# Where the low part of the transposed x is formed: VectorE from PSUM instead of GpSimd from SBUF

## The chip, the cores and the metric

The kernel runs on one core of a Trainium2 chip. The time is the device time of one execution in microseconds (us); the median of three executions of the kernel before is 827.89 us. Engines are called TensorE, VectorE, ScalarE, GpSimd and SyncE; in the rows of the profile they are PE (with PEld, its weight loads), DVE, ACT, POOL and SP.

## The reference

x has 32 batches of 256 tokens of 128 features. Three layers follow one another, each added to x:

```python
x = x + 0.5 * ffn(layernorm(x), router_w, w1, w2)      # stream f1
x = x + attn(layernorm(x), W_qkv, W_out)               # stream at
x = x + 0.5 * ffn(layernorm(x), router_w, w1, w2)      # stream f2

# ffn: 8 experts of widths 4 x 128 and 4 x 256, all computed, the best two of a token weighted
probs = sigmoid(x @ router_w.T); topw, sel = top_k(probs, 2); topw /= topw.sum() + 1e-20
h = square(relu(x @ w1[e])); y = h @ w2[e]; out = sum over e of y * combine[e]
# attn: linear attention, 16 heads of 8, with rotary embedding and the feature map elu + 1
```

## The kernel before

The tokens are worked through in 16 groups of 512 tokens (two batches). Each group goes through the streams f1, at and f2. One pass `iteration(t, par)` of the software pipeline, written out by hand for every engine, works on different groups in the different streams: f1 forms the inputs of group t + 2, attention those of group t - 1, and f2 those of group t + 2 - 5. t runs from -3 to 22. Up to t = 3 only f1 has work among the two ffn streams (the ramp), from t = 14 only f2 (the drain); the ten passes between have both.

For precision a product of two float32 matrices is made of three products in TensorE's fp32r format: high part by high part, low by high, high by low. So the transposed and normalised x of a group needs a high part `x_hi` (the value rounded to fp32r) and a low part `x_lo` (the value minus `x_hi`), each 128 x 512. They are made so, for each of the three streams:

1. TensorE (`transpose`) writes the four transposed tiles into PSUM bank 0, called `tp` (L474).
2. ScalarE (`evacuate_x`) copies `tp` to `xT` in SBUF (L721), once `x_lo` of the group before in line has been formed, since all streams share one `xT`.
3. VectorE (`high_part`) casts `xT` to `x_hi` (L978).
4. GpSimd (`low_part`) subtracts `x_hi` from `xT` and gives `x_lo` (L876).

For the ffn streams TensorE (`logits`, L493) then multiplies `xT` by the router's weights and writes the result into the same bank `tp`. ScalarE takes the exponential of it (`exp_logits`, L730 and L734). The router's weights of the tokens are worked out on VectorE, with a square root on GpSimd (`root_of_weights`, L882), turned round through `tp` again (`weight_rows`, L483), written to DRAM, and broadcast by SyncE's DMAs from there to `g_all`, four pieces to a group.

The hidden layer has 12 chunks of 128 units to a group and stream. A pass has 24 places. In the passes with both streams each place has one chunk; where a stream is alone its chunks stand at every second place. A chunk goes: three matmuls on TensorE (`up`, L512 to L514) into one of two banks; VectorE multiplies by the router's weights (`weighted`, L1060, `hid`); ScalarE squares (L752) and rounds to `h_hi` (L763); GpSimd forms `h_lo` (`remainders`, L888); nine places later three matmuls `down` (L530 to L532) add it up.

Each engine does its list strictly in the written order. What matters here:

- TensorE: transpose f1, places 0 to 2, `logits` f1, places 3 to 8, transpose at, places 9 to 11, transpose f2, places 12 to 14, q, `logits` f2, and so on.
- VectorE: `weighted(t, 0)`, `high_part` f1, `weighted(t, 1)`, ..., `mean_variance` f1 after place 4; `high_part` at after place 10; `high_part` f2 after place 12. The first `weighted` of a stream waits for the first piece of `g_all` of its group.
- ScalarE: `exp_logits` f1 stands ahead of `squares(t, 0)`, and `exp_logits` f2 ahead of `squares(t, 4)`.
- GpSimd: `low_part` f1 between the `h_lo` of places 22 and 23 of the pass before; `inv_std` f1 (L864 to L869, 1/std of the layernorm of group t + 3) after the `h_lo` of place 1; `low_part` at after place 7, f2 after place 10.

Of the kernel before, what the change touches and what calls it, by code (L numbers as in the profile page):

```python
# [27 lines left out]
F32 = mybir.dt.float32  # L28
F32R = mybir.dt.float32r
ALU = mybir.AluOpType  # L30
ACT = mybir.ActivationFunctionType
# [5 lines left out]
BG = 2  # L37
# [26 lines left out]
SHIFT = 5  # L64
T_FIRST, T_LAST = -3, NG + SHIFT

class Step:
# [14 lines left out]
    @property  # L82
    def last(self):
        return self.c + self.a * (self.trips - 1)

    @property
    def value(self):
        return self.i * self.a + self.c


def first(v):
    return v.c if isinstance(v, Step) else v
# [10 lines left out]
def due(v):  # L103

    assert (first(v) > 0) == (last(v) > 0)
    return first(v) > 0


def live(n):

    return first(n) >= 0 and last(n) < NG


def first_time(stream, n):

    return stream and not isinstance(n, Step) and n == 0


def done(n):

    if last(n) <= 0:
        return 0
    if first(n) >= NG:
        return NG
    assert first(n) >= 0 and last(n) <= NG
    return n
# [66 lines left out]
def build(nc, x_in, wqkv, wout, router, w1, w2, const, out, rows):  # L193
    ctx = ExitStack()
    with ctx:
        def sb(name, shape, dt=F32):
            return ctx.enter_context(nc.sbuf_tensor(name, shape, dt))

        def sem(name):
            return ctx.enter_context(nc.semaphore(name))  # L200
# [29 lines left out]
        xT = sb("xT", [P, NTOK])  # L230
        xT = {s: xT for s in STREAMS}
        nx = {"f1": 2, "at": 1, "f2": 2}
        x_hi = {s: [sb(f"x_hi_{s}{u}", [P, NTOK], F32R) for u in range(nx[s])] for s in STREAMS}
        x_lo = {s: [sb(f"x_lo_{s}{u}", [P, NTOK], F32R) for u in range(nx[s])] for s in STREAMS}
# [52 lines left out]
        tp = bank[0]  # L287
# [16 lines left out]
        def per(name, keys):  # L304
            return {s: sem(f"s_{name}_{s}") for s in keys}
# [8 lines left out]
        s_xT = per("xT", STREAMS)  # L314
        s_hi = per("hi", STREAMS)
        s_lo = per("lo", STREAMS)
# [28 lines left out]
        A = {n: sem(f"s_a_{n}") for n in names}  # L345
# [104 lines left out]
        def _(pe):  # L450
            mm = nc.tensor.matmul

            def tp_free(t, pos):

                n = [done(m + (pos > k)) for k, m in
                     enumerate((t + 2, t + 1 - SHIFT, t - 1, t + 2 - SHIFT, t + 2))]
                if due(n[0]):
                    pe.wait_ge(s_ex["f1"], value(n[0]))
                if due(n[1]):
                    pe.wait_ge(s_gr["f2"], value(n[1]))  # L460
                if due(n[2]):
                    pe.wait_ge(s_xT["at"], value(n[2]))
                if due(n[3]):
                    pe.wait_ge(s_ex["f2"], value(n[3]))
                if due(n[4]):
                    pe.wait_ge(s_gr["f1"], value(n[4]))
# [19 lines left out]
            def logits(s, n):  # L486
                if not live(n):
                    return
                pe.wait_ge(s_xT[s], value(n + 1))
                if first_time(s == "f1", n):  # L490
                    pe.wait_ge(s_router, 16)
                for k in range(TG):
                    i = mm(tp[:, k * P:k * P + PAD], xT[s][:, k * P:(k + 1) * P], router_sb[:], start=True, stop=True)  # L493
                i.then_inc(s_logit[s], 1)
# [192 lines left out]
        def _(act):  # L687
            fn = nc.scalar.activation
# [23 lines left out]
            def evacuate_x(s, n, t, pos):  # L712
                if not live(n):
                    return
                act.wait_ge(s_t[s], value(n + 1))

                for q, m in (("f1", t + 2), ("at", t - 1), ("f2", t + 2 - SHIFT)):
                    m = done(m + 1 if STREAMS.index(q) < pos else m)
                    if due(m):
                        act.wait_ge(s_lo[q], value(m))  # L720
                fn(xT[s][:], tp[:], ACT.Copy).then_inc(s_xT[s], 1)  # L721

            def exp_logits(s, n):
                if not live(n):
# [122 lines left out]
        @block.gpsimd  # L847
        def _(pool):
            gp = nc.gpsimd
            gp.memset(router_sb[:], 0.0).then_inc(s_zero, 1)  # L850
            gp.memset(c_eps[:], EPS)
            gp.memset(c_mhalf[:], -0.5)
            gp.memset(c_half[:], 0.5)
            gp.memset(c_one[:], 1.0)
            gp.memset(c_cut[:], -ROOT_CUT)
            gp.memset(c_mone[:], -1.0).then_inc(s_pconst, 1)
            pool.wait_ge(s_pconst, 1)

            def inv_std(s, n):

                if not live(n):
                    return
                pool.wait_ge(s_mv[s], value(n + 1))
                gp.tensor_tensor(ve[s][:], mv[s][:, :, 1], c_eps[:], ALU.add).then_inc(s_ve[s], 1)  # L864
                gp.tensor_tensor(nm[s][:], mv[s][:, :, 0], c_mone[:], ALU.mult).then_inc(s_ve[s], 1)
                pool.wait_ge(s_ve[s], value(n * 2 + 2))
                gp.tensor_tensor(rstd[s][:], ve[s][:], c_mhalf[:], ALU.pow).then_inc(s_rstd[s], 1)
                pool.wait_ge(s_rstd[s], value(n + 1))
                gp.tensor_tensor(nbias[s][:], nm[s][:], rstd[s][:], ALU.mult).then_inc(s_nb[s], 1)  # L869

            def low_part(s, n, par):
                if not live(n):
                    return
                u = par if nx[s] == 2 else 0
                pool.wait_ge(s_hi[s], value(n + 1))
                gp.tensor_tensor(x_lo[s][u][:], xT[s][:], x_hi[s][u][:].bitcast(F32), ALU.subtract).then_inc(s_lo[s], 1)  # L876

            def root_of_weights(s, n):
                if not live(n):
                    return  # L880
                pool.wait_ge(s_cwt[s], value(n + 1))
                gp.tensor_tensor(root[s][:], cwt[s][:], c_half[:], ALU.pow).then_inc(s_root[s], 1)  # L882

            def remainders(t, *places):
                for place in places:
                    for s, n, c, _ in chunks(t, place):
                        pool.wait_ge(s_hhi[s], value(n * NC + c + 1))
                        gp.tensor_tensor(h_lo[:, c, :], hid[:, c % STAGE, :], h_hi[:, c, :].bitcast(F32),  # L888
                                         ALU.subtract).then_inc(s_hlo[s], 1)

            def iteration(t, par):
                remainders(t - 1, 21, 22)
                low_part("f1", t + 2, par)
                remainders(t - 1, 23)
                if first_time(True, t + 2):
                    pool.wait_ge(s_w2hi, 1)
                    gp.tensor_tensor(w2_lo[:], w2_raw.rearrange("p (c d) -> p c d", c=NC),
                                     w2_hi[:].bitcast(F32), ALU.subtract).then_inc(s_w2lo, 1)
                remainders(t, 0, 1)
                inv_std("f1", t + 3)  # L900
                remainders(t, 2, 3, 4, 5, 6)
                root_of_weights("f1", t + 2)
                remainders(t, 7)
                low_part("at", t - 1, 0)
                remainders(t, 8, 9, 10)
                low_part("f2", t + 2 - SHIFT, (par + SHIFT) % 2)
                remainders(t, 11)
                remainders(t, 12, 13, 14, 15)
                inv_std("at", t)
                remainders(t, 16, 17, 18)  # L910
                root_of_weights("f2", t + 2 - SHIFT)
                remainders(t, 19)
                inv_std("f2", t + 3 - SHIFT)
                remainders(t, 20)

            pipeline(pool, iteration)


        @block.vector
        def _(dve):  # L920
            v = nc.vector
# [48 lines left out]
                    i = v.bn_aggr(mv[s][:, k, :], bn[s][:, k, :])  # L970
                i.then_inc(s_mv[s], 1)

            def high_part(s, n, par):
                if not live(n):
                    return
                u = par if nx[s] == 2 else 0
                dve.wait_ge(s_xT[s], value(n + 1))
                v.tensor_copy(x_hi[s][u][:], xT[s][:]).then_inc(s_hi[s], 1)  # L978


            def take_sigmoid(s, n):

# [179 lines left out]
            def iteration(t, par):  # L1162
                p2 = (par + SHIFT) % 2
                n1, n2, n2_last = t + 2, t + 2 - SHIFT, t + 1 - SHIFT
# [4 lines left out]
                k_features(t - 2)  # L1169
                q_features(t - 2)  # L1170
                weighted(t, 0)
                high_part("f1", n1, par)
                spread_roots("f2", n2_last, 0)
                weighted(t, 1)
                spread_roots("f2", n2_last, 1)
# [21 lines left out]
                weighted(t, 9)  # L1197
                normalise(t - 2, 2)
                weighted(t, 10)
                high_part("at", t - 1, 0)  # L1200
                choose_two("f1", n1)
                weighted(t, 11)
                weighted(t, 12)
                high_part("f2", n2, p2)
                spread_roots("f1", n1, 0)
                weighted(t, 13)
                spread_roots("f1", n1, 1)
# [62 lines left out]
```

## Time and profile before

| what | us |
|---|---|
| median of 3 executions | 827.89 (826.98 to 828.34) |
| the profiled execution | 823.68 |
| its span, first to last instruction | 821.5 |
| TensorE busy | 737.2 (90%) |
| GpSimd busy | 685.2 (83%) |
| ScalarE busy | 599.2 (73%) |
| VectorE busy | 588.3 (72%) |
| mean granted TensorE clock | 0.978 of full |

Busy time is the time in which the engine had an instruction under way. The profiled execution has 2.2 us outside its span.

### The profile page before, as it was taken

How to read it: one execution, taken by the hardware profiler on the slowest of the kernel's cores; microseconds unless marked ns; L12 is line 12 of the kernel's file. 1: busy time of each engine (PE TensorE's matmuls, PEld its weight loads, DVE VectorE, ACT ScalarE, POOL GpSimd, SP SyncE). 2: the span in 40 equal slices, each digit the busy share in tenths (PEclk: the TensorE clock that was granted, in tenths of full speed). 3: DMA queues.
4: the chain of work that ended last, by engine and by line, in shares of the span. 5: the costliest groups of instructions: out<-in, count | busy, mean ns of one | idle time of the engine just before them, and what ended most of it. 6: DMA issues, size and time to landing. Idle time of an engine off the chain costs nothing.

```text
span 821.5 us, 14132 instructions
## 1 busy us (share of the span) xinstructions
PE 737.2 (90%) x3648; PEld 598.1 (73%) x3648; DVE 588.3 (72%) x1820; ACT 599.2 (73%) x1219; POOL 685.2 (83%) x668
## 2 busy tenths in 40 slices
PE   1679888889999999999899998999999989789887
PEld 1457666767887888878687886878887868667665
DVE  3454678777879798887679687787888577676553
ACT  3567686667787879787687877788877765766765
POOL 4587868869999999999799997999989877675876
PEclk9998999989999999999999999999999999989999
DMA  5443023023233331312333230223333303303330
GB/s 173 167 156 115 28 104 104 1 103 104 104 105 116 104 118 67 107 56 106 108 103 116 103 116 21 107 92 103 117 104 117 116 2 104 94 24 117 116 116 26
DMA packets 31009, 79.25 MB, mean 96 GB/s; under 512 B 3296, under 2 KB 14304, under 8 KB 30944
## 3 DMA queue, kind: packets, MB, share of 16 engines
q1 hardware_dynamic: 28672, 76.03, 27.2%
q10 hardware_dynamic: 2272, 2.51, 0.9%
q8 instruction: 22, 0.36, 0.2%
q14 instruction: 43, 0.35, 0.1%
HBM read 73.81 MB, written 4.72 MB: 96 GB/s over the span
## 4 chain that ended last, share of the span: by engine, by line
PE 45%; POOL 15%; DVE 13%; issue 12%; ACT 10%; DMA 4%; DVEq 0%; POOLq 0%; ACTq 0%; SPq 0%
POOL h_lo L888 9%; PE bank L512 6%; PE bank L530 5%; PE bank L514 5%; PE bank L513 5%; PE bank L531 5%; PE bank L532 5%; DVE hid L1060 4%; ACT h_hi L763 3%; PE bank L563 3%; DMA g_all_f<-rows_f 3%; PE bank L493 2%; ACT hid L752 2%; PE bank L614 2%; ACT xn_f L709 2%
## 5 line engine op out<-in xcount | busy, mean ns | idle before, releaser
L888 POOL TENSOR_TENSOR h_lo<-hid,h_hi 128x512 fp32r<-128x512 f32 x384 | 493.8, 1309 | 97.0 <-ACT h_hi L763 96.3
L1060 DVE SCALAR_TENSOR_TENSOR hid<-bank,g_all_f 128x512 f32<-128x512 f32 x384 | 262.2, 684 | 155.2 <-PE bank L514 121.9
L752 ACT ACTIVATE hid<-hid 128x512 f32<-128x512 f32 x384 | 228.8, 621 | 47.9 <-DVE hid L1060 47.3
L763 ACT ACTIVATE h_hi<-hid 128x512 fp32r<-128x512 f32 x384 | 225.5, 620 | 4.3
L512 PE MATMUL bank<-x_hi_f,w_hi 128*128 128x512 f32 x384 | 165.7, 431 | 21.5 <-DVE hid L1060 20.3
L530 PE MATMUL bank<-h_hi,w_hi 128*128 128x512 f32 x384 | 156.9, 409 | 17.8 <-ACT yT L774 10.6
L531 PE MATMUL bank<-h_lo,w_hi 128*128 128x512 f32 x384 | 153.9, 401 | 0.0
L514 PE MATMUL bank<-x_hi_f,w_lo 128*128 128x512 f32 x384 | 153.7, 400 | 0.0
L532 PE MATMUL bank<-h_hi,w_lo 128*128 128x512 f32 x384 | 153.4, 399 | 0.0
L513 PE MATMUL bank<-x_lo_f,w_hi 128*128 128x512 f32 x384 | 152.9, 398 | 0.0
L512 PEld LDWEIGHTS bank<-x_hi_f,w_hi 128*128 128x128 f32 x384 | 73.9, 192 | 48.0 <-DVE hid L1060 29.7
L530 PEld LDWEIGHTS bank<-h_hi,w_hi 128*128 128x128 f32 x384 | 73.8, 192 | 40.9 <-POOL h_lo L888 14.6
L514 PEld LDWEIGHTS bank<-x_hi_f,w_lo 128*128 128x128 f32 x384 | 73.3, 191 | 17.9
L532 PEld LDWEIGHTS bank<-h_hi,w_lo 128*128 128x128 f32 x384 | 73.5, 192 | 17.1
L531 PEld LDWEIGHTS bank<-h_lo,w_hi 128*128 128x128 f32 x384 | 73.8, 192 | 15.9
L513 PEld LDWEIGHTS bank<-x_lo_f,w_hi 128*128 128x128 f32 x384 | 73.9, 193 | 11.1
L709 ACT ACTIVATE xn_f<-x_sb,nbias_f,rstd_f 128x128 f32<-128x128 f32 (+1 forms) x128 | 52.4, 481 | 11.5 <-POOL nbias_f L869 11.5
L876 POOL TENSOR_TENSOR x_lo_f<-xT,x_hi_f 128x512 fp32r<-128x512 f32 x32 | 41.4, 1292 | 18.7 <-DVE x_hi_f L978 18.7
L882 POOL TENSOR_TENSOR root_f<-cwt_f,c_half 128x8 f32<-128x8 f32 x32 | 53.5, 1672 | 0.0
L721 ACT ACTIVATE xT<-bank 128x512 f32<-128x512 f32 x48 | 28.4, 593 | 31.8 <-PE bank L474 21.2
L978 DVE CAST x_hi_f<-xT 128x512 fp32r<-128x512 f32 x32 | 21.9, 683 | 31.6 <-ACT xT L721 31.6
L730 ACT ACTIVATE ex_f<-bank 128x32 f32<-128x32 f32 x32 | 6.4, 199 | 50.4 <-PE bank L493 50.4
(106 smaller groups left out, 1055.2 us busy)
## 6 DMA issues: line engine op xcount, KB each, us to landing
g_all_f<-rows_f SPq DMA_DIRECT2D x128, 512.0 KB, 5.2
x_sb<-in_x SPq DMA_DIRECT2D x16, 256.0 KB, 3.8
out_x<-x_sb SPq DMA_DIRECT2D x16, 256.0 KB, 6.8
g_all_f<-in_w ACTq DMA_DIRECT2D x2, 768.0 KB, 7.2
con<-in_const ACTq DMA_DIRECT2D x1, 652.0 KB, 7.4
rows_f<-g_row_f SPq DMA_DIRECT2D x32, 16.0 KB, 1.4
g_all_f<-in_wqkv ACTq DMA_DIRECT2D x1, 192.0 KB, 9.2
wout_sb<-in_wout ACTq DMA_DIRECT2D x1, 64.0 KB, 6.9
```

Source lines behind the costliest of these rows:

```text
L512: mm(o, w1_hi[:, w], x_hi[s][u][:], start=True, stop=False)
L513: mm(o, w1_hi[:, w], x_lo[s][u][:], start=False, stop=False)
L514: mm(o, w1_lo[:, w], x_hi[s][u][:], start=False, stop=True).then_inc(s_p1[s], 1)
L530: mm(o, w2_hi[:, c, :], h_hi[:, c, :], start=(c == 0), stop=False)
L531: mm(o, w2_hi[:, c, :], h_lo[:, c, :], start=False, stop=False)
L532: i = mm(o, w2_lo[:, c, :], h_hi[:, c, :], start=False, stop=(c == NC - 1))
L709: i = fn(xn[s][:, k, :], tile, ACT.Identity, bias=nbias[s][:, k:k + 1], scale=rstd[s][:, k:k + 1])
L752: fn(h, h, ACT.Square).then_inc(s_sq[s], 1)
L763: fn(h_hi[:, c, :], hid[:, c % STAGE, :], ACT.Copy).then_inc(s_hhi[s], 1)
L882: gp.tensor_tensor(root[s][:], cwt[s][:], c_half[:], ALU.pow).then_inc(s_root[s], 1)
L888: gp.tensor_tensor(h_lo[:, c, :], hid[:, c % STAGE, :], h_hi[:, c, :].bitcast(F32), ALU.subtract).then_inc(s_hlo[s], 1)
L1060: v.scalar_tensor_tensor(hid[:, c % STAGE, :], hp[c % 2][:], 0.0, g_all[s][:, EXPERT[c], :], ALU.max, ALU.mult).then_inc(s_z[s], 1)
```

## The change

- `x_lo` is now formed by VectorE: it subtracts `x_hi` from the PSUM bank `tp` itself, right behind the place where it made `x_hi`. GpSimd's `low_part` is gone.
- In the stream at, ScalarE writes the rounded `x_hi` straight from `tp`, instead of `xT`; VectorE's cast of that stream is gone. ScalarE then waits for the key and value products of the attention group before, which read `x_hi`.
- Since `tp` is now read by VectorE too, `logits` waits for `x_lo` of its stream and group, and the users of `tp` that come after the transposes of the stream at wait for its `x_lo` in place of its `xT`.

```diff
                 if due(n[2]):
-                    pe.wait_ge(s_xT["at"], value(n[2]))
+                    pe.wait_ge(s_lo["at"], value(n[2]))
...
                 pe.wait_ge(s_xT[s], value(n + 1))
+                pe.wait_ge(s_lo[s], value(n + 1))
                 if first_time(s == "f1", n):
...
-                fn(xT[s][:], tp[:], ACT.Copy).then_inc(s_xT[s], 1)
+                if s == "at":
+                    if due(n):
+                        act.wait_ge(A["kv"], value(n * BG))
+                    fn(x_hi[s][0][:], tp[:], ACT.Copy).then_inc(s_hi[s], 1)
+                else:
+                    fn(xT[s][:], tp[:], ACT.Copy).then_inc(s_xT[s], 1)
...
-            def low_part(s, n, par):
-                if not live(n):
-                    return
-                u = par if nx[s] == 2 else 0
-                pool.wait_ge(s_hi[s], value(n + 1))
-                gp.tensor_tensor(x_lo[s][u][:], xT[s][:], x_hi[s][u][:].bitcast(F32), ALU.subtract).then_inc(s_lo[s], 1)
-
...
-                low_part("f1", t + 2, par)
...
-                low_part("at", t - 1, 0)
...
-                low_part("f2", t + 2 - SHIFT, (par + SHIFT) % 2)
...
-            def high_part(s, n, par):
+            def split_x(s, n, par):
                 if not live(n):
                     return
                 u = par if nx[s] == 2 else 0
-                dve.wait_ge(s_xT[s], value(n + 1))
-                v.tensor_copy(x_hi[s][u][:], xT[s][:]).then_inc(s_hi[s], 1)
-
+                if s != "at":
+                    dve.wait_ge(s_xT[s], value(n + 1))
+                    v.tensor_copy(x_hi[s][u][:], xT[s][:]).then_inc(s_hi[s], 1)
+                dve.wait_ge(s_hi[s], value(n + 1))
+                v.tensor_tensor(x_lo[s][u][:], tp[:], x_hi[s][u][:].bitcast(F32), ALU.subtract).then_inc(s_lo[s], 1)
...
-                high_part("f1", n1, par)
+                split_x("f1", n1, par)
...
-                high_part("at", t - 1, 0)
+                split_x("at", t - 1, 0)
...
-                high_part("f2", n2, p2)
+                split_x("f2", n2, p2)
```

## Rows read from the trace of the kernel before

**Rows 1.** Windows: stretch, busy us (instructions) of PE, PEld, DVE, ACT, POOL, granted clock, DMA

```profile
65.00:68.00 3.00, 3.00 (x10) 2.40 (x9) 0.82 (x2) 1.26 (x2) 3.00 (x3) 0.50 0.21 71
...
240.00:280.00 40.00, 39.47 (x203) 32.64 (x202) 33.16 (x109) 31.70 (x69) 38.52 (x39) 1.00 0.22 75
```

**Rows 2.** Who waited for whom: total us, times, longest

```profile
PE bank L512 <- DVE hid L1060: 20.3, 26, 3.6
...
PE bank L530 <- POOL h_lo L888: 7.2, 10, 2.7
...
PEld bank L563 <- POOL x_lo_at L876: 0.7, 2, 0.4
```

**Rows 3.** Instructions by line, shapes apart: busy us, mean ns

```profile
L876 POOL TENSOR_TENSOR x_lo_f<-xT,x_hi_f 128x512 fp32r<-128x512 f32 x32 | 41.4, 1292 | 18.7 <-DVE x_hi_f L978 18.7
...
L876 POOL TENSOR_TENSOR x_lo_at<-xT,x_hi_at 128x512 fp32r<-128x512 f32 x16 | 20.7, 1292 | 0.0
```

**Rows 4.** Single lines: duration ns min/median/max, first and last start

```profile
L978 DVE CAST x_hi_f<-xT x32: 409/717/1514, 14.9 to 775.0; 128x512 fp32r<-128x512 f32 x32
L978 DVE CAST x_hi_at<-xT x16: 415/418/1539, 92.4 to 714.5; 128x512 fp32r<-128x512 f32 x16
...
L1077 DVE TENSOR_TENSOR qa<-bank,con x16: 672/676/682, 96.4 to 719.3; 128x512 f32<-128x512 f32 x16
```

**Rows 5.** Timeline, a pass with both streams, 264 to 290 us: start, us, instruction [idle before]

```profile
264.44 0.50 DVE L978 CAST x_hi_f<-xT 128x512 fp32r<-128x512 f32 x1
...
264.57 0.50 PE L512 MATMUL bank<-x_hi_f,w_hi 128*128 128x512 f32 x1 [0.38 <-DVE hid L1060]
...
266.97 1.03 PE L493 MATMUL bank<-router_sb,xT 128*128 128x96 f32 x8
...
286.45 0.60 ACT L721 ACTIVATE xT<-bank 128x512 f32<-128x512 f32 x1 [0.68 <-POOL x_lo_at L876]
...
287.08 0.74 DVE L978 CAST x_hi_f<-xT 128x512 fp32r<-128x512 f32 x1 [2.12 <-ACT xT L721]
...
289.04 1.02 PE L493 MATMUL bank<-router_sb,xT 128*128 128x96 f32 x8
```

**Rows 6.** Timeline of the ramp, pass t = 0, 51 to 63 us

```profile
51.84 1.03 PE L493 MATMUL bank<-router_sb,xT 128*128 128x96 f32 x8
...
53.20 0.32 ACT L734 ACTIVATE odds_f<-ex_f,c_one 128x32 f32<-128x32 f32 x1
...
54.62 0.69 DVE L1060 SCALAR_TENSOR_TENSOR hid<-bank,g_all_f 128x512 f32<-128x512 f32 x1 [5.09 <-DMA g_all_f<-rows_f]
...
55.22 0.42 DVE L978 CAST x_hi_f<-xT 128x512 fp32r<-128x512 f32 x1
55.34 0.63 ACT L752 ACTIVATE hid<-hid 128x512 f32<-128x512 f32 x1 [1.82 <-DVE hid L1060]
...
58.77 0.20 POOL L864 TENSOR_TENSOR ve_f<-mv_f,c_eps 128x4 f32<-128x4 f32 x1
...
62.78 0.77 PE L530 MATMUL bank<-h_hi,w_hi 128*128 128x512 f32 x1 [3.66 <-ACT yT L774]
```

**Rows 7.** Timeline of passes t = 1 and t = 2: logits, cast, first square

```profile
79.15 1.02 PE L493 MATMUL bank<-router_sb,xT 128*128 128x96 f32 x8
...
80.90 0.71 DVE L978 CAST x_hi_f<-xT 128x512 fp32r<-128x512 f32 x1
...
81.02 0.64 ACT L752 ACTIVATE hid<-hid 128x512 f32<-128x512 f32 x1 [0.19 <-DVE hid L1060]
...
108.60 1.51 DVE L978 CAST x_hi_f<-xT 128x512 fp32r<-128x512 f32 x1
...
109.16 1.03 PE L493 MATMUL bank<-router_sb,xT 128*128 128x96 f32 x8
```

**Rows 8.** Timeline of the last router pass, 772 to 776 us

```profile
772.86 1.03 PE L493 MATMUL bank<-router_sb,xT 128*128 128x96 f32 x8
...
775.03 0.42 DVE L978 CAST x_hi_f<-xT 128x512 fp32r<-128x512 f32 x1
```

## The prediction

> **What bounds the kernel now.** I read the busy time by stretches first. In a stretch of the ten passes with both streams TensorE has 39.47 us busy of 40, GpSimd 38.52, VectorE 33.16 and ScalarE 31.70 [rows 1]. So in the middle of the run TensorE sets the pace, and GpSimd stands only a little behind it. Then the waits: in the whole run TensorE waits 7.2 us for GpSimd's `h_lo` ahead of L530, its weight loads 0.7 us for `x_lo` of the stream at, and 20.3 us for VectorE's `hid` ahead of L512 [rows 2]. What GpSimd costs TensorE directly is small, whatever its busy share.
>
> The timeline shows where the rest is. In the ramp and the drain a pass is one chain of single steps, with TensorE idle in it: logits, exponential on ScalarE, square and rounding of the first chunk, `h_lo` and 1/std on GpSimd, the next norm and `yT` on ScalarE, and TensorE, which had waited 3.66 us for that [rows 6]. There a late step is paid in full. The reader should see in rows 6 above all that TensorE does the logits at 51.84, ScalarE is done with the exponential at 53.52, and only then, at 54.62, does VectorE get past its wait of 5.09 us for the broadcast of the router's weights. The cast to `x_hi` stands behind that wait, at 55.22. Nobody but GpSimd's `low_part` needed it earlier.
>
> **The change, part by part.** *GpSimd.* It loses 32 + 16 subtractions of 1292 ns, 41.4 + 20.7 = 62.1 us, 3.9 us in a full pass [rows 3]. TensorE can get back from this at most what it waits for GpSimd, 7.2 + 0.7 = 7.9 us if every such wait went [rows 2]. Only few of these waits stand behind a subtraction: I take 1 us, the queue of `h_lo`, root and `x_lo_at` ahead of q in the second attention pass, and keep 0 and 7.9 as ends.
>
> *VectorE.* It gains 48 subtractions with one operand in PSUM. The trace has none; the nearest row is the multiplication of a bank by a constant of the same size, 676 ns, never below 672 or above 682 [rows 4]. I take 0.68 us, and 0.07 us for its wait for the cast just ahead. It loses 16 casts of the stream at, 415 to 1539 ns [rows 4]. In a full pass that is 3 x 0.68 = 2.0 us more, less 0.4 to 1.5. The casts' spread comes from GpSimd: a cast from SBUF that meets one of its 1.3 us subtractions stands until that is done, the multiplication from PSUM never does [rows 4]. I take it that the subtraction is not held up either; if it were, it would cost up to 1539 - 415 = 1124 ns more where it meets one, which is kept as an end of the range for the waits in the ramp. The Trainium skill has a rule on this (SBUF — State Buffer, SBUF: two separate sides): VectorE and GpSimd share a port pair under an exclusive lock, which VectorE needs in its two-port mode or with two SBUF inputs. By that rule the subtraction, with one input in SBUF, is free of the lock, and its 0.68 us would stand; a design that kept the subtraction in SBUF on VectorE would not have that. The row of L1077 agrees.
>
> *ScalarE.* It copies as many times as before, with another output type. I take nothing: the wait for the old key and value products is over half a pass old when it is reached, and the rounding copy to `h_hi` costs as much as the square beside it.
>
> *TensorE.* This is the part that costs. `logits` had to wait for `xT` only; it now waits for `x_lo`, because it overwrites the bank that VectorE still reads. Behind it on TensorE stand the next `down` and `up` chunks, behind them `hid` and VectorE's statistics. On ScalarE `exp_logits` waits for it, and behind that, in order, stand all squares of the pass. On the path to GpSimd's 1/std the squares come first.
>
> In the passes with both streams there is slack. f1: the cast ends at 264.94, `x_lo` at 264.94 + 0.75 = 265.69, the logits start at 266.97, 1.3 us later. f2: 287.82 + 0.75 = 288.57 against 289.04, 0.47 us; besides, ScalarE's copy had waited 0.68 us for GpSimd's `x_lo_at` and now comes that much earlier, so the slack grows to about 1.1 us [rows 5]. The transposes of f2 wait for `x_lo` of at, about 1.3 us ahead of need. TensorE's own bubble in such a pass is 0.38 us behind the first `hid` [rows 5]; with the ten passes it could give 4 us at most, and nothing here removes its cause, the attention features ahead of that `hid`. I take 0, with -4 and +7 as ends (the latter if f2 loses 0.7 us in each of ten passes).
>
> In the ramp there is none. From the start of the logits to the end of `odds` takes 53.52 - 51.84 = 1.68, so the first square can start 1.7 us after `x_lo` is ready [rows 6].
> - t = 0: `x_lo` at 55.22 + 0.42 + 0.75 = 56.39, first square at 58.1 instead of 55.34: +2.75 [rows 6].
> - t = -1: the same pattern (logits at 28.3, broadcast landed at 30.2): +2.75.
> - t = 1: 80.90 + 0.71 + 0.75 = 82.36, square at 84.06 instead of 81.02: +3.0 [rows 7].
> - t = 2: 108.60 + 1.51 + 0.75 = 110.86, logits due at 109.16; ScalarE's squares followed at once: +1.7 [rows 7].
> - t = 3: the same with a cast of 1.14: +1.3.
>
> The sum for the ramp is 11.5 us. In the drain the last router pass has the pattern of t = 0: the logits at 772.86 wait for 775.03 + 0.42 + 0.75 = 776.2 [rows 8], first square +2.75. The pass before it loses 0.9, and in two passes the transposes of f2 wait 0.5 each for `x_lo` of at, together 1.9. All in all 11.5 + 2.75 + 1.9 = 16.2 us. Against it stand the 1 us of GpSimd's queue and, as an estimate, 2 us of delays that fall into waits still there (of the 3.66 and similar): the delay of one step is not always that of the pass. That leaves +13.2 us: the profiled 823.7 would become 836.9. The median of the runs lies 4.2 above the profiled execution, so 827.9 + 13.2 = 841 us.
>
> *The clock.* After TensorE had waited 3.66 us at 62.78 it was granted 0.50, the 1.2 GHz level, through 65 to 68 us [rows 1, 6], and its matmuls ran at half pace. With the change its idle time in t = -1, 0 and 1 is cut differently: about 4.5 us idle ahead of the logits, then work, then the old wait. If each of the four large waits brings one more such stretch, of 5 us at half pace, that is 4 x 2.5 = 10 us more. This is in the range, not in the sum. A rule of the Trainium skill speaks for it (TensorE: Matmul & The Clock Gate, Part 1: The HAM clock gate): idleness lets the gate fall to 1.2 GHz, and activity releases it. By the trace it fell at such a wait; whether the split wait makes more or fewer falls no row shows.
>
> **The rivals.**
> *Slower by about 1.6%* is the forecast, with the waits of the logits paid on the chain. Chance 0.68.
> *Slower by much more*: the same, with the extra half-clock stretches or with VectorE as the late engine in every full pass: 841 + 10 = 851 us or 841 + 7 = 848. For it: rows 1 show the clock falling after such a wait. Against it: the slacks of rows 5. Chance 0.14.
> *The waits are absorbed*: TensorE waits in these passes anyway, so a logits that starts late only moves its idle time, and GpSimd's relief pays the rest. That holds if the first square, not the logits, waits for something later. It doesn't by rows 6 to 8, where the square starts within 0.1 us of VectorE's `hid`, but the steps behind could have slack unseen: +0 to +3, about 829 us. Chance 0.08, half of it within 0.2%.
> *Faster*: GpSimd at 38.5 of 40 us is the true bound of the full passes, and what the rows name as waits for VectorE comes from it at one remove (held-up casts and features). Then a full pass wins the 0.38 us and more, ten passes 4 us, and the ramp part of the 7.9 us, while the logits wait costs less than 3 us in all: 827.9 - 4 - 4 + 3 = 823 us. It decides if VectorE reaches the cast before the logits are due; in rows 6 to 8 it reaches it 0.6 us before to 3.4 us after. Chance 0.10.
>
> **How the numbers follow.** The likeliest case gives 841 us, its own range 835 to 847. To hold 8 in 10 the range reaches up to the clock case and down to where most of the delay is absorbed: 832 to 851. A difference of 0.2% (1.7 us) is about what a measurement of this kernel can tell from none. Slower by more: 0.68 + 0.14 + 0.04 = 0.86; within: 0.04; faster: 0.10.
>
> **What would show it.** In the profile after: the logits of t = -1, 0 and 1 begin right after VectorE's subtraction and TensorE waits for it, some 3 to 4.5 us each; `odds` and the first square follow 1.7 us later. The subtraction takes 0.68 us everywhere. GpSimd falls to about 623 us busy, VectorE rises to about 588 + 33 - 13 = 608. A full pass stays as long as before. The prediction is wrong if full passes get shorter by more than 0.4 us each, if the subtraction is held up, or if the ramp ends as early as before though its logits wait.

## The result, and the profile after

The median of 20 executions is 835.77 us (831.44 to 842.31), against 828.26 us of the kernel before, measured beside it in 20 executions. The ratio is 1.0099, with a 95% interval of 1.0078 to 1.0119: slower by 8.2 us (6.5 to 9.9). Forecast were +13.2 us and a range of 832 to 851. The profiled execution took 834.58 us, its span 832.8.

The page of the kernel after, busy time and two of its groups, with the idle time of the engine ahead of each:

```profile
PE 739.5 (89%) x3648; PEld 599.9 (72%) x3648; DVE 601.9 (72%) x1852; ACT 596.7 (72%) x1219; POOL 622.6 (75%) x620
...
L494 PE MATMUL bank<-router_sb,xT 128*128 128x96 f32 x256 | 36.5, 289 | 18.4 <-DVE x_lo_f L977 16.5 <-issue 1.9
...
L977 DVE TENSOR_TENSOR x_lo_f<-bank,x_hi_f 128x512 fp32r<-128x512 f32 x32 | 22.1, 692 | 1.1
```

GpSimd has lost 63 us of busy time, VectorE gained 14. GpSimd's work is gone as forecast, and the kernel is slower: its busy share had cost little. What is new is the first group's idle time. TensorE now waits 16.5 us ahead of the logits (L494, L493 before) for VectorE's `x_lo`. The timeline says where:

```profile
31.81 1.99 PE L494 MATMUL bank<-router_sb,xT 128*128 128x96 f32 x8 [3.53 <-DVE x_lo_f L977]
58.70 1.10 PE L494 MATMUL bank<-router_sb,xT 128*128 128x96 f32 x8 [3.71 <-DVE x_lo_f L977]
85.66 1.10 PE L494 MATMUL bank<-router_sb,xT 128*128 128x96 f32 x8 [3.15 <-DVE x_lo_f L977]
116.55 1.10 PE L494 MATMUL bank<-router_sb,xT 128*128 128x96 f32 x8 [1.67 <-DVE x_lo_f L977]
147.81 1.10 PE L494 MATMUL bank<-router_sb,xT 128*128 128x96 f32 x8 [1.31 <-DVE x_lo_f L977]
...
758.69 1.10 PE L494 MATMUL bank<-router_sb,xT 128*128 128x96 f32 x8 [0.81 <-DVE x_lo_f L977]
785.26 1.10 PE L494 MATMUL bank<-router_sb,xT 128*128 128x96 f32 x8 [2.32 <-DVE x_lo_f L977]
```

These are the passes t = -1 to 3 of the ramp and the last two router passes of the drain, and none of the passes between. The 1.9 us that the group's row puts down to "issue" stand ahead of the very first logits (t = -2), which start at 16.27 instead of 14.96; the first `x_lo` ends at 16.2, so this wait too is most likely one for `x_lo`. Pass t = 0 after, timeline of several engines, to be read beside [rows 6]:

```profile
56.80 0.69 DVE L1058 SCALAR_TENSOR_TENSOR hid<-bank,g_all_f 128x512 f32<-128x512 f32 x1 [4.29 <-DMA g_all_f<-rows_f]
57.41 0.42 DVE L975 CAST x_hi_f<-xT 128x512 fp32r<-128x512 f32 x1
57.86 0.69 DVE L977 TENSOR_TENSOR x_lo_f<-bank,x_hi_f 128x512 fp32r<-128x512 f32 x1
...
60.13 0.32 ACT L740 ACTIVATE odds_f<-ex_f,c_one 128x32 f32<-128x32 f32 x1
60.36 1.13 ACT L758 ACTIVATE hid<-hid 128x512 f32<-128x512 f32 x2
...
67.49 0.47 PE L531 MATMUL bank<-h_hi,w_hi 128*128 128x512 f32 x1 [1.91 <-ACT yT L780]
```

From the first `hid` to the first square there were 0.72 us, and now there are 3.56: 2.84 more, where the prediction had 2.75. But the whole step from one broadcast's arrival to the next grew only from 25.7 to 26.3 us (the first `hid` of pass t = 1 is at 83.08, of t = 0 at 56.80; before, 80.29 and 54.62). From the first `hid` to the end of TensorE's wait for `yT` it is 10.7 us instead of 8.2, and from there to the next `hid` 15.6 instead of 17.5. The clock gave that back. Windows after:

```profile
60.00:65.00 5.00, 5.00 (x17) 3.92 (x16) 2.18 (x13) 3.70 (x8) 2.67 (x5) 0.66 0.65 207
67.00:72.00 5.00, 4.51 (x22) 3.75 (x23) 2.02 (x7) 3.91 (x8) 3.65 (x4) 1.00 0.25 80
```

The half-clock stretch now lies ahead of the wait for `yT`, where TensorE has time; behind it, where before it ran at 0.50 [rows 1], it has the full 2.4 GHz.

### The profile page after: what moved, and what is told of

It reads as the page before. It is cut to its first block, busy times and chain, and to the rows that moved or that the text cites. A ratio compares the mean times of both kernels' runs of the same rounds, so it can differ in the third digit from the quotient of the medians.

```text
span 832.8 us, 14152 instructions
## 1 busy us (share of the span) xinstructions
PE 739.5 (89%) x3648; PEld 599.9 (72%) x3648; DVE 601.9 (72%) x1852; ACT 596.7 (72%) x1219; POOL 622.6 (75%) x620
## 3 DMA queue, kind: packets, MB, share of 16 engines
q1 hardware_dynamic: 28672, 76.03, 26.3%
## 4 chain that ended last, share of the span: by engine, by line
PE 59%; DVE 17%; issue 8%; ACT 7%; POOL 5%; DMA 4%; DVEq 0%; POOLq 0%; ACTq 0%; SPq 0%
PE bank L513 8%; PE bank L515 7%; PE bank L514 7%; PE bank L531 7%; PE bank L532 7%; PE bank L533 7%; DVE hid L1058 5%; PE bank L564 4%; PE bank L494 4%; DMA g_all_f<-rows_f 2%; POOL h_lo L887 2%; PE bank L627 2%; PE bank L615 2%; ACT xn_f L710 2%; ACT h_hi L769 2%
## 5 line engine op out<-in xcount | busy, mean ns | idle before, releaser
L494 PE MATMUL bank<-router_sb,xT 128*128 128x96 f32 x256 | 36.5, 289 | 18.4 <-DVE x_lo_f L977 16.5
L494 PEld LDWEIGHTS bank<-router_sb,xT 128*128 128x128 f32 x256 | 35.0, 207 | 22.4 <-issue 21.2
L975 DVE CAST x_hi_f<-xT 128x512 fp32r<-128x512 f32 x32 | 32.3, 1010 | 19.1 <-ACT xT L727 19.1
```

## The experiments

Each was timed side by side with the kernel before. The ratios stand with their 95% intervals.

| kernel | median us | ratio | interval |
|---|---|---|---|
| the change | 835.77 | 1.0099 | 1.0078 to 1.0119 |
| x1: only the stream at | 824.27 | 0.9963 | 0.9942 to 0.9984 |
| x2: only f1 and f2 | 840.44 | 1.0166 | 1.0133 to 1.0198 |
| x3: f1 and f2 from SBUF | 839.62 | 1.0165 | 1.0129 to 1.0201 |
| x4: split ahead of the first hid | 822.60 | 0.9943 | 0.9922 to 0.9964 |
| x5: x4, and at in the drain | 820.78 | 0.9922 | 0.9893 to 0.9952 |
| x6: before, with x4's order | 825.52 | 0.9983 | 0.9962 to 1.0004 |
| x7: f1, f2 by stage | 824.39 | 0.9962 | 0.9945 to 0.9979 |
| x8: x4 only behind the broadcast | 826.46 | 0.9982 | 0.9959 to 1.0006 |
| x9: before, logits wait for x_lo | 907.03 | 1.0934 | 1.0901 to 1.0968 |

The profiled executions by stage, in us. The ramp is taken up to the logits of f1 in t = 4, the full stage is the nine passes from there to the logits of f1 in t = 13, and the drain is the rest:

| kernel | ramp | nine full passes | drain | span |
|---|---|---|---|---|
| before | 177.3 | 411.2 | 233.0 | 821.5 |
| the change | 182.8 | 412.4 | 237.6 | 832.8 |
| x1 | 175.5 | 411.1 | 235.8 | 822.4 |
| x3 | 176.2 | 423.7 | 236.7 | 836.6 |
| x4 | 172.4 | 411.3 | 238.0 | 821.7 |
| x5 | 169.7 | 407.1 | 239.6 | 816.3 |
| x6 | 174.2 | 415.5 | 234.3 | 824.0 |
| x8 | 171.2 | 411.0 | 237.8 | 820.0 |
| x9 | 200.4 | 454.9 | 253.2 | 908.5 |

This is one execution of each, and the executions of the kernel before lie between 823.6 and 832.2 us. Before and x6 have the same code in the full passes and are 4 us apart there, so that a smaller difference in a stage is not shown by this table alone.

**x1 and x2, the halves.** x1 has the change's edits for at, and f1 and f2 as before; x2 the other way round.

```diff
 # x1, against the change: GpSimd's low_part is back for f1 and f2 at its old places, and
-                pe.wait_ge(s_lo[s], value(n + 1))          # in logits
...
                     v.tensor_copy(x_hi[s][u][:], xT[s][:]).then_inc(s_hi[s], 1)
+                    return
...
```

> Only the stream at is changed: ScalarE writes its high part, VectorE subtracts from PSUM; f1 and f2 stay with GpSimd and their logits don't wait. Theory H (the loss comes from the logits waiting while VectorE still needs the bank): nothing of the 8 us of loss is left, and the 0.3 us that each full pass gained may stay: 825 to 828 us. Rival V (VectorE's longer list is what costs): also 825 to 828, so this run alone doesn't part them; it says whether the stream at gains or loses anything. A loss of over 2 us would mean that the transposes of f2 waiting for the low part of at cost something.

> Only f1 and f2 are changed, the stream at is as before. H: the whole loss is here, 8 to 11 us, 836 to 839 us, and TensorE waits ahead of the logits as in the full change (16.5 us in seven places). If the two halves of the change work on each other (ScalarE's copy for f2 waiting for GpSimd's low part of at), the loss is larger still, since the f2 logits have 0.5 us of slack only: up to 843.

x1 is 3 us faster than before (1.3 to 4.8), x2 13.7 slower (11 to 16). So the stream at is a gain, and the loss is all in f1 and f2. In x2 TensorE waits more than in the full change:

```profile
L494 PE MATMUL bank<-router_sb,xT 128*128 128x96 f32 x256 | 38.5, 300 | 21.7 <-DVE x_lo_f L981 19.7 <-issue 1.9
```

It is 19.7 us in ten places. The three new ones are f2 logits (1.38, 0.70 and 0.69 us), where ScalarE's copy for f2 still waits for GpSimd's `x_lo` of at. The halves do work on each other.

**x3, the bank let go.** VectorE does the same subtractions at the same places, but from the copy in SBUF, so that the logits needn't wait.

```diff
-                pe.wait_ge(s_lo[s], value(n + 1))          # in logits
...
-                v.tensor_tensor(x_lo[s][u][:], tp[:], ...
+                v.tensor_tensor(x_lo[s][u][:], tp[:] if s == "at" else xT[s][:], ...
```

> The full change, but VectorE subtracts for f1 and f2 from the copy in SBUF, so the logits need not wait for it. VectorE's list is as long as in the full change, or longer where GpSimd holds it up. H: 825 to 829 us, no wait of TensorE ahead of the logits. V: 834 us or more, as VectorE does the same work at the same places.

By its time the rival V would have won, and H missed by over 10 us. The rows show another mechanism than the one that V was to explain, the loss of the change. The waits ahead of the logits are gone, and the ramp is no longer than before: the logits of t = 4 start at 176.24, against 182.81 in the change. The full passes are what became longer. x3, groups by line, the subtraction's shortest, median and longest duration in ns, and the f1 logits of two full passes in line:

```profile
L976 DVE TENSOR_TENSOR x_lo_f<-xT,x_hi_f 128x512 fp32r<-128x512 f32 x32 | 42.4, 1324 | 1.1
...
L976 DVE TENSOR_TENSOR x_lo_f<-xT,x_hi_f x32: 691/1647/1673, 15.4 to 790.1; 128x512 fp32r<-128x512 f32 x32
...
268.59 1.03 PE L493 MATMUL bank<-router_sb,xT 128*128 128x96 f32 x8
...
315.05 1.03 PE L493 MATMUL bank<-router_sb,xT 128*128 128x96 f32 x8
```

With both operands in SBUF the subtraction takes 1324 ns on average instead of 692, and an ordinary full pass 46.5 us instead of 44.4 (below). The nine full passes together are 11.3 us longer than in the change, since not all of them grew by 2 us. The average hides two cases. Eleven of the 32 subtractions, all in ramp and drain, run while GpSimd does nothing and take 691 ns, as from PSUM; the other 21 run beside GpSimd's `h_lo` and take 1.64 to 1.67 us. So what the PSUM operand buys is that GpSimd can't hold the subtraction up; holding the bank is its price. That agrees with the rule on the shared port pair in the Trainium skill (SBUF — State Buffer, SBUF: two separate sides), by which two SBUF inputs need the lock against GpSimd.

**x4, the same work earlier.** In the change the split stands behind a `hid` that waits for the broadcast. x4 puts it ahead, where only f1 runs, and in the last router pass of f2.

```diff
+                if alone("f1", t):
+                    split_x("f1", n1, par)
                 weighted(t, 0)
-                split_x("f1", n1, par)
+                if not alone("f1", t):
+                    split_x("f1", n1, par)
...
+                if early:                                  # the last group of f2
+                    split_x("f2", n2, p2)
                 weighted(t, 12)
...
```

> The full change, with VectorE's split of x ahead of the first hid where f1 is alone, and in the last pass of f2: no longer behind the wait for the broadcast. H with the broadcast as its cause: the waits of TensorE ahead of the logits of t = -1, 0, 1 and the last one (3.5, 3.7, 3.2 and 2.3 us) go, those of t = 2 and 3 shrink, and the time falls to 827 to 830 us. V: it stays at 835.

The kernel falls from 1.0099 to 0.9943, 4 us below the lower end expected. Of the waits ahead of the logits two are left, in the drain:

```profile
748.82 1.10 PE L494 MATMUL bank<-router_sb,xT 128*128 128x96 f32 x8 [0.82 <-DVE x_lo_f L977]
774.25 1.10 PE L494 MATMUL bank<-router_sb,xT 128*128 128x96 f32 x8 [1.10 <-DVE x_lo_f L977]
```

16.5 - 1.9 = 14.6 us of waits went, and 1.0099 - 0.9943 = 1.56% or 12.9 us of time. VectorE's list is as long as in the change, so its length is not what costs. By stage the gain lies in the ramp: 13.4 us of waits went there, and the profiled ramp is 10.4 us shorter than that of the change. The drain is not shorter (238.0 against 237.6). There only 1.2 us of waits went, and 3.2 us are left: 0.82 and 1.10 ahead of the logits and twice 0.64 ahead of the transposes of f2, for the `x_lo` of at. So x4 says little of the 3 to 5 us by which the drain of the change is longer than those of x6 and before. x1 and x3, whose logits don't wait, lie between (235.8 and 236.7). That fits waits that are paid in the drain too, but these differences are no larger than those between executions.

**x6, the control,** and **x8, the waits apart.** x6 is the kernel before with the cast moved as in x4. x8 is x4 with the split moved only up to t = 1 and in the last pass of f2.

```diff
 # x8, against x4
-                if alone("f1", t):
+                first = not isinstance(t, Step) and t <= 1
+                if first:
                     split_x("f1", n1, par)
...
```

> Control for x4: the kernel before, with only the order on VectorE changed in the same passes (cast ahead of the first hid). If x4 is faster than before because of where the low part is formed, this stays at 828, as nobody on the chain waited for the cast. If the order alone gains, by GpSimd's low part and the h_lo queued behind it coming earlier, it goes to 823 to 825, and x4's gain is not that of the change.

> As x4, but the split stands ahead of the first hid only where that hid waited for the broadcast (up to t = 1, and the last pass of f2); in t = 2 and 3 it is behind it as in the full change. If each wait ahead of the logits is paid at about its length: x4 plus the waits of t = 2 and 3 (1.7 + 1.3), 825.5 us. If the passes behind the broadcast were the cheap ones and t = 2 and 3 the dear ones: 830 or more. If waits of 1.5 us are absorbed: 823.

x6 can't be told from before; at most 3.1 us come from the order alone, 1.4 us is its middle. In x8 the waits are 1.46 and 1.30 us in t = 2 and 3. It stands 0.39% or 3.2 us above x4, for 2.8 us of waits, and 1.17% or 9.7 us below the change, for 11.6 us of waits (3.53 + 3.71 + 3.15 + 1.22). By the middles a microsecond of waiting ahead of the logits costs 0.8 to 1.2 us, with room to both sides, since each interval is 0.2% wide either way. For the small step the profiles don't bear it out: the ramp of x8 is no longer than that of x4 (171.2 and 172.4 us), so that the 3.2 us rest on the medians alone. From the change to x4, less the 1.4 us of x6, it is 11.5 us for 14.6.

**x5, the low part of at as well.**

```diff
+                if alone("f2", t):
+                    split_x("at", t - 1, 0)
                 weighted(t, 10)
...
```

> The kernel of x4, and in the drain the low part of the stream at also goes ahead of the hid of place 10, so that the transposes of f2 no longer wait for it. If these waits (about 0.6 us in each of two passes) are on the chain: 821 to 822 us, 1 us less than x4. If they lie in slack, or if the hid that comes 0.7 us later is what the chain runs through: 822.6 or up to 1.5 more.

820.78 us is the fastest version, 0.78% under before (0.48 to 1.07). Against x4 the intervals overlap, so that this last step gained is not shown. Its profiled drain is no shorter than x4's (239.6 and 238.0 us), and there two f2 logits now wait 0.32 us each.

**x7, VectorE only in the full passes.** at as in the change; f1 and f2 by `on_vector(s, t)`, false where f1 or f2 is alone.

```diff
+        def on_vector(s, t):
+            return s == "at" or not (alone("f1", t) or alone("f2", t))
...
```

> Stream at on VectorE throughout; f1 and f2 on VectorE only in the ten passes with both streams, on GpSimd in ramp and drain. By the theory that the logits' waits in ramp and drain are the whole loss: no such waits, full passes of 44.4 us, 823 to 825 us as x1. If VectorE's two more subtractions cost something in the full passes that the waits of the change had covered: 827 or more.

0.9962, the same as x1. In the full passes it makes no difference who forms the low part of f1 and f2, once at is on VectorE.

**x9, the wait alone.** One line more in the kernel before; GpSimd still forms `x_lo`.

```diff
                 pe.wait_ge(s_xT[s], value(n + 1))
+                pe.wait_ge(s_lo[s], value(n + 1))
```

> The kernel before with one line more: the logits also wait for the low part, which GpSimd still forms. Theory H: the wait alone costs, and here more than in the full change, since GpSimd's low part comes later than VectorE's: about 0.6 us more in the ramp, and in a full pass, from the rows before, x_lo of f1 at 268.57 against logits due at 266.97 (1.6 us) and of f2 at 291.46 against 289.04 (2.4 us). 13 + 3 in ramp and drain and up to 10 x 4 in the full passes: 845 to 884 us. If it stays under 836, what the full change loses is not the wait.

It took 907 us, 23 more than the upper end expected. x9, who waited for whom, three logits in line, and windows over two passes:

```profile
PE bank L494 <- POOL x_lo_f L877: 65.8, 28, 4.7
...
373.38 1.10 PE L494 MATMUL bank<-router_sb,xT 128*128 128x96 f32 x8 [2.41 <-POOL x_lo_f L877]
...
399.20 1.10 PE L494 MATMUL bank<-router_sb,xT 128*128 128x96 f32 x8 [1.58 <-POOL x_lo_f L877]
...
423.92 1.10 PE L494 MATMUL bank<-router_sb,xT 128*128 128x96 f32 x8 [2.42 <-POOL x_lo_f L877]
...
299.74:348.66 48.92, 44.65 (x228) 36.67 (x229) 36.43 (x113) 36.45 (x76) 42.62 (x42) 1.00 0.27 93
348.66:399.20 50.54, 46.16 (x228) 37.80 (x229) 36.87 (x113) 36.68 (x76) 42.63 (x42) 0.97 0.25 90
```

The waits in a full pass, 2.42 and 1.58 us, are what the rows before had given (2.4 and 1.6). A pass took 48.9 us instead of 44.8 where the clock stayed at full, 4.1 more for 4.0 of waiting, and 50.5 us where it was granted 0.97: there TensorE was busy 1.5 us longer with the same matmuls. So in the full passes a wait costs its length, and the clock comes on top in some of them. Over the whole profiled execution the mean granted clock is 0.948, against 0.978; the medians over all executions are 0.954 and 0.970.

## Why the prediction was right, and where it was off

**The waits.** *"`logits` ... now waits for `x_lo`, because it overwrites the bank that VectorE still reads"* is what costs in the ramp: x4 takes it away with all the rest in place, and its profiled ramp is 10.4 us shorter. That it is also what lengthens the drain fits the runs and is not shown by them. The five places in the ramp and the two in the drain are those named. The first three are 0.1 to 0.8 us shorter than the start times had given (3.7, 4.55 and 3.2), since other steps of the chain had come later too; their effect on the first square was met to 0.1 us in t = 0.

**The sum of the waits** was 16.2 us less 2 for what is absorbed, 14.2. Taking 14.6 us of them away gave 11.5 us (x4 less x6), so the price of a wait was about right. What the prediction did not have is what came back behind them. The profiled execution of the change is 8.9 us late at the first logits of f2 (164.09 against 155.19), and only 5.5 us late one step on, at the f1 logits of t = 4. Windows over this step, before and after:

```profile
155.19:177.26 22.07, 17.30 (x76) 14.03 (x76) 19.76 (x61) 11.77 (x24) 16.54 (x19) 0.85 0.26 97
```

```profile
164.09:182.81 18.72, 14.26 (x77) 11.39 (x75) 17.18 (x59) 11.55 (x24) 12.29 (x16) 1.00 0.33 114
```

TensorE did the same matmuls in 14.26 us instead of 17.30, at a clock of 1.00 instead of 0.85. Before, it had waited 1.79 us for attention's `x_sb` in this step, and after 0.26. Whether GpSimd's relief or the shifted times kept the clock up is open: the step takes 21.2 us in x6, 19.9 in x1 and 18.7 in x4. In t = 0, too, the absorption came from the clock, and not from slack behind the chain. The clock rival, four more half-clock stretches, did not come: the mean clock is 0.977 as before (0.978), and the medians over all executions are 0.971 and 0.970.

**The full passes** are a second term that was mis-sized. The prediction said *"I take 0"* and *"nothing here removes its cause"*. An ordinary full pass became 0.3 us shorter. Logits of f1 in two passes in line, before and after (44.75 and 44.43 us):

```profile
222.22 1.03 PE L493 MATMUL bank<-router_sb,xT 128*128 128x96 f32 x8
```

```profile
272.21 1.03 PE L494 MATMUL bank<-router_sb,xT 128*128 128x96 f32 x8
...
316.64 1.03 PE L494 MATMUL bank<-router_sb,xT 128*128 128x96 f32 x8
```

The first fence belongs to the 266.97 of [rows 5]. The bubble of 0.38 us, which was looked at, is still there. Another one went: before, TensorE also waited at the end of the pass. VectorE, GpSimd and TensorE before, then after, at the same place:

```profile
299.37 3.83 POOL L888 TENSOR_TENSOR h_lo<-hid,h_hi 128x512 fp32r<-128x512 f32 x3
...
302.40 0.88 DVE L1028 TENSOR_TENSOR chosen_f<-which_f,con 128x64 f32<-128x64 uint32 x1
...
305.93 0.49 PE L512 MATMUL bank<-x_hi_f,w_hi 128*128 128x512 f32 x1 [0.17 <-DVE hid L1060]
```

```profile
304.31 3.82 POOL L887 TENSOR_TENSOR h_lo<-hid,h_hi 128x512 fp32r<-128x512 f32 x3
...
307.64 0.57 DVE L1026 TENSOR_TENSOR chosen_f<-which_f,con 128x64 f32<-128x64 uint32 x1
...
310.87 0.49 PE L513 MATMUL bank<-x_hi_f,w_hi 128*128 128x512 f32 x1
```

`chosen`, a VectorE operation of 192 ns at its shortest, had stood 0.88 us beside GpSimd and now stands 0.57. Both times it ends 0.08 us after GpSimd's run of three `h_lo` (303.20 and 308.13), and that run ends 0.31 us earlier in its pass after the change. Step by step the two passes of TensorE run alike up to this matmul, and 0.30 us apart from it on. That is the small version of the rival *faster*: GpSimd holding up VectorE at one remove. Ten such passes would give 3 us, which is also x1's gain, though the 0.17 us of TensorE's wait alone would have shown only half of it. The nine passes of the two profiled executions don't show the sum, 411.2 before and 412.4 after. Two of the nine are longer than the others in both kernels (49.6 and 48.0 us before, 49.8 and 49.7 after), each with a stop of VectorE of 3.3 us or more that the profile puts down to issue. In these the granted clock was 0.97 and 1.00 before, 0.94 and 0.95 after. Against x6, with the same full passes as before, the change is 3.0 us shorter there. That `chosen` is shorter because GpSimd's queue stands otherwise at that moment is read from the two timelines; no run moved it alone.

**The account.** The measured +8.2 is 5 us under the forecast. By stage, forecast and then measured in the profiled execution against before and against x6: ramp +11.5, measured +5.5 and +8.6; full passes 0, measured +1.2 and -3.0; drain +4.65, measured +4.6 and +3.2. Off the sum the prediction took 3 us that it put to no stage. So the ramp came out smaller than its waits, in part by what the clock gave back (3.0 us of TensorE's busy time in the one step above), and the full passes are at most 3 us of the difference. How the 5 us divide between the two is not shown, as single executions differ by as much. The drain came out at about its size, but no run parts its cause from the spread of the executions.

**Smaller points.** The subtraction takes 692 and 681 ns (taken: 680), never held up in 48 places: right. GpSimd has 622.6 us busy (forecast 623), VectorE 601.9 (608). f2's slack in the full passes came out smaller than the 1.1 us forecast, as its cast now runs beside GpSimd's `h_lo` and takes 1.35 us instead of 0.74; there were still 0.7 us left. The transposes of f2 wait 1.3 us in all for `x_lo` of at (forecast 1.0).

## What to carry to other kernels

An operation that reads PSUM in place of a copy in SBUF holds the bank: look for the next writer of that bank, and at what stands ahead of the reader in its own engine's list, above all a wait for a DMA. With a pipeline that fills and drains, check these stages apart from the full one; here an ordinary full pass gained 0.3 us, and ramp and drain together lost 10 us in the profiled executions. Where such a move loses, try the order first: two calls moved turned 1% slower into 0.6% faster. And look in which stage a cure helps: here it was the ramp, and the drain stayed as long.

## What the runs showed of the hardware

The same 128 x 512 subtraction on VectorE took 692 ns with one operand in PSUM, whatever GpSimd did. With both operands in SBUF (x3) it took 691 ns in the eleven places where GpSimd did nothing and 1.64 to 1.67 us in the 21 places where `h_lo` ran beside it. And one wait of about 2 us, put twice into each pass of a kernel whose TensorE was 98.7% busy in the full passes (39.47 of 40 us), cost 9.3% (x9): 65.8 us of waits became 78 us of time. Where the granted clock stayed at 1.00, 4.0 us of waits made a pass 4.1 us longer; at 0.97 it was 5.7 us.
